# Another on-chip layout for the expert stage of a layer kernel, and another order of its 16 last x1 loads

## The reference

```python
x = x + layernorm(scan_layer(layernorm(x)))      # a state-space scan, 16 states per channel
x = x + layernorm(moe(layernorm(x)))             # 8 experts, top 2, and a shared expert

# moe, for each of the two choices k:
    pos = running count of the tokens that chose expert e;  keep = pos < 640
    h = gelu(buf @ w1[e] + b1[e]);  y = h @ w2[e] + b2[e] + gelu(buf @ wd[e]) @ wu[e]
    out += y[token's slot] * keep * weight
out += 0.2 * (gelu(x @ sw1 + sb1) @ sw2 + sb2 + gelu(x @ swd) @ swu)
```

## Time and profile before

| | us |
|---|---|
| median of 3 runs | 3554.31 (3552.27 to 3554.70) |
| the profiled execution | 3554.31 |
| its span, first to last instruction | 3552.6 |
| TensorE busy | 3143.4 (88%) |
| VectorE busy | 1853.6 (52%) |
| ScalarE busy | 1425.1 (40%) |
| GpSimd busy | 1727.5 (49%) |

### The profile page before, as it was taken

One profiled execution on the slowest core, in us unless ns is written; L12 is line 12 of the kernel. 1 busy time (PEld: TensorE's weight loads), 2 busy tenths in 40 slices (PEclk: granted clock), 3 DMA queues, 4 the chain that ended last, 5 costly groups with the idle time before them and its releaser, 6 DMA issues.

```text
span 3552.6 us, 43069 instructions
## 1 busy us (share of the span) xinstructions
PE 3143.4 (88%) x15191; PEld 2576.9 (73%) x15191; DVE 1853.6 (52%) x2708; ACT 1425.1 (40%) x2529; POOL 1727.5 (49%) x1577
## 2 busy tenths in 40 slices
PE   6455699988999988889999999999999999999991
PEld 3233577777777776678888888888888888888881
DVE  6699989988899981462322232223222322232225
ACT  7554676666766763312221321322313213223113
POOL 1087787987879874432341532613514416235102
PEclk8655799999999999879999999999999999999996
DMA  8859688696886945821230321412303314123036
GB/s 260 246 167 246 176 224 215 207 267 181 233 215 207 269 139 174 265 68 22 66 80 16 95 63 26 112 27 63 84 15 93 65 18 115 32 60 83 16 83 225
DMA packets 276920, 463.42 MB, mean 130 GB/s; under 512 B 32065, under 2 KB 107729, under 8 KB 276706
## 3 DMA queue, kind: packets, MB, share of 16 engines
q1 hardware_dynamic: 206656, 266.21, 26.5%
q0 software_dynamic: 68288, 194.06, 21.1%
q10 hardware_dynamic: 1762, 0.40, 0.1%
HBM read 363.44 MB, written 97.14 MB: 130 GB/s over the span
## 4 chain that ended last, share of the span: by engine, by line
PE 53%; DVE 2%; DMA 2%; issue 1%; POOL 1%; ACT 1%; SPq 0%; POOLq 0%; DVEq 0%; ACTq 0%
PE c_psH L1774 26%; PE c_psY L1818 25%; PE c_psT L1765 1%; PE c_psT L1869 1%; DMA raw<-in_w 1%; DVE d_y L1745 1%; DVE d_st L1729 1%; PE c_psY L1814 0%; DVE yst L1541 0%; DMA xrow<-x_d 0%; DMA acc_d<-yst,slot_lists 0%; POOL W1l L1411 0%; POOL acc_d L1456 0%; POOL W2l L1411 0%; ACT h L1325 0%
## 5 line engine op out<-in xcount | busy, mean ns | idle before, releaser
L1557 DVE CAST hh<-h 128x512 fp32r<-128x512 f32 (+1 forms) x400 | 177.0, 443 | 1257.1 <-ACT h L1331 1227.2
L1331 ACT ACTIVATE h<-c_psH,biases 128x512 f32<-128x512 f32 (+1 forms) x400 | 248.2, 621 | 1283.7 <-PE c_psH L1774 1260.1
L829 POOL TENSOR_TENSOR u<-dtxs,Bt 128x512 f32<-128x512 f32 x512 | 659.1, 1309 | 167.5 <-DVE b_psA L732 146.9
L732 DVE TENSOR_TENSOR_SCAN b_psA<-b_psA,b_few,u 128x512 f32<-128x512 f32 x512 | 656.9, 1283 | 63.8 <-ACT b_psA L602 61.2
L937 PE MATMUL b_psY<-ident,pr 128*128 128x128 f32 x2048 | 349.8, 310 | 210.7 <-DVE pr L739 192.1
L1818 PE MATMUL c_psY<-W2h,hh 128*128 128x512 f32 x1344 | 535.0, 398 | 0.6
L1818 PE MATMUL c_psY<-W2l,hh 128*128 128x512 f32 x1344 | 525.7, 391 | 0.0
L1818 PE MATMUL c_psY<-W2h,hl 128*128 128x512 f32 x1344 | 524.6, 390 | 0.0
L1416 POOL DMA_INDIRECT xrow<-xt_d,slot_lists x80 | 91.8, 1147 | 843.5 <-PE c_psT L1765 442.3
L937 PEld LDWEIGHTS b_psY<-ident,pr 128*128 128x128 f32 x2048 | 268.1, 157 | 295.1 <-DVE pr L739 242.6
L739 DVE TENSOR_TENSOR pr<-b_psA,Ct 128x512 f32<-128x512 f32 x512 | 354.3, 692 | 19.8 <-DMA Ct<-bc_d 2.0
(11 more groups left out here) (260 smaller groups left out, 5826.2 us busy)
## 6 DMA issues: line engine op xcount, KB each, us to landing
w<-ws_d POOLq DMA_DIRECT2D x224, 512.0 KB, 6.3
raw<-in_w SPq DMA_DIRECT2D x256, 256.0 KB, 2.8
Bt<-bc_d SPq DMA_DIRECT2D x64, 512.0 KB, 15.5
Ct<-bc_d SPq DMA_DIRECT2D x64, 512.0 KB, 19.6
xn<-in_x SPq DMA_DIRECT2D x8, 1024.0 KB, 6.9
xT_d<-xnT SPq DMA_DIRECT2D x8, 1024.0 KB, 8.4
dt_d<-a_dt SPq DMA_DIRECT2D x8, 1024.0 KB, 7.3
dtx_d<-a_dx SPq DMA_DIRECT2D x8, 1024.0 KB, 7.6
```

The lines of the kernel that those rows point to most:

```text
L732: nc.vector.tensor_tensor_scan(psA[q][:, :], psA[q][:, :], u[g % U_RING][:, :], carry[:, k:k + 1], ALU.mult, ALU.add).then_inc(s_h, 1)
L829: nc.gpsimd.tensor_tensor(u[g % U_RING][:, :], dtx[s % 2][:, :], Bt[n // TG][:, n % TG, :], ALU.mult)\
L1331: nc.scalar.activation(h32[:, 0:n * P], psH[j % 2][:, 0:n * P], ACT.Gelu, bias=b1[:, j - 1:j]).then_inc(s_gelu, 1)
```

## The change

It has two parts. First, the tiles of `experts` are opened in another order. The small tiles and Xb now come first, then the router's scratch tiles (closed again), and over the same bytes Xa, Xc and then the four weight tiles; after those are closed the tail's statistics tiles, `x1r` and `y` are laid over Xa, Xc and the weights together. The first byte of the tiles in a partition, summed up from the declarations:

| tile | before | after |
|---|---|---|
| L1h / L1l | 224,512 / 226,176 | 17,664 / 19,328 |
| Xbh / Xbl | 148,736 / 156,928 | 23,040 / 31,232 |
| Xah / Xal | 199,936 / 208,128 | 73,600 / 81,792 |
| Xch / Xcl | 216,320 / 220,416 | 89,984 / 94,080 |
| W1h / W1l | 17,664 / 50,432 | 98,176 / 130,944 |
| W2h / W2l | 83,200 / 115,968 | 163,712 / 196,480 |
| x1r[0] | 17,664 | 75,008 |
| y[0] | 83,200 | 140,544 |
| ident, the identity for transposes | 16,512 | 16,512 |
| skip_diagonal, of `mix` | 17,664 | 17,664 |

`x1r[0]` to `x1r[4]` now lie over Xa and Xc, `x1r[5]` begins in Xcl and reaches into W1h, `x1r[6]` to `x1r[12]` lie in W1h, `x1r[13]` lies across W1h and W1l, `x1r[14]` and `x1r[15]` in W1l. Second, the waits of SyncE in front of the loads of `x1r` follow this: groups 0 to 4 wait for the end of block 1, group 5 for 3 finished `up` of the last block, group 6 for 5, and so on to group 11 for 15, and groups 12 to 15 for all 17. The loads of `y` and their waits stay.

```diff
--- before.py
+++ after.py
@@ -1037,13 +1037,9 @@
         def sb(name, shape, dt=F32, where=ctx):
             return where.enter_context(nc.sbuf_tensor(name, shape, dt))
 
-        loop = ExitStack()
-        W1h, W1l = (sb(f"W1{h}", [P, FC, DT, P], F32R, loop) for h in "hl")
-        W2h, W2l = (sb(f"W2{h}", [P, FC, D], F32R, loop) for h in "hl")
-        loop.close()
-        x1r, y = ([sb(f"d_{n}{g}", [P, TAIL_G, D]) for g in range(NT // TAIL_G)] for n in ("x1", "y"))
+        L1h, L1l = sb("L1h", [P, DT, L3 + E], F32R), sb("L1l", [P, DT, L3 + E], F32R)
+        L2 = sb("L2", [L3, D], F32R)
         Xb = (sb("Xbh", [P, DT, 512], F32R), sb("Xbl", [P, DT, 512], F32R))
-        L2 = sb("L2", [L3, D], F32R)
         h32 = sb("h32", [P, 512])
         hh = [sb(f"hh{q}", [P, 512], F32R) for q in range(2)]
         hl = [sb(f"hl{q}", [P, 512], F32R) for q in range(2)]
@@ -1051,6 +1047,13 @@
         xrow = [sb(f"xrow{q}", [P, D]) for q in range(2)]
         yst = [sb(f"yst{q}", [P, D]) for q in range(4)]
         b2bc = sb("b2bc", [P, D])
+        biases = sb("biases", [P, (E + 2) * FC])
+        b1T, b1e = biases[:, 0:(E + 1) * FC], biases[:, (E + 1) * FC:(E + 2) * FC]
+        slots = sb("slot_rows", [P, 2, E * ST])
+        slot_g, slot_s = slots[:, 0, :], slots[:, 1, :]
+        few = sb("slot_lists", [P, LINE])
+        idx, sidx = few[:, 0:ST].bitcast(I32), few[:, ST:2 * ST].bitcast(I32)
+        wsl = few[:, 2 * ST:3 * ST]
         rt = ExitStack()
         OH = sb("OH", [P, K, NT, E], F32, rt)
         RA = sb("RA", [P, K, NT, E], F32, rt)
@@ -1073,20 +1076,16 @@
         hl_f = RA[:, :, :, :].rearrange("p k t e -> p (k t e)")[:, 0:2 * K * NT]\
             .rearrange("p (h k t) -> p h k t", h=2, k=K)
         rt.close()
-        end = ExitStack()
-        st, mv = (sb(f"d_{n}", [P, NT, m], F32, end) for n, m in (("st", 6), ("mv", 2)))
-        sd, rs, nm = (sb(f"d_{n}", [P, NT], F32, end) for n in ("sd", "rs", "nm"))
-        end.close()
-        Xa = (sb("Xah", [P, DT, 512], F32R), sb("Xal", [P, DT, 512], F32R))
-        X = (Xa, Xb, (sb("Xch", [P, DT, 256], F32R), sb("Xcl", [P, DT, 256], F32R)))
-        L1h, L1l = sb("L1h", [P, DT, L3 + E], F32R), sb("L1l", [P, DT, L3 + E], F32R)
-        biases = sb("biases", [P, (E + 2) * FC])
-        b1T, b1e = biases[:, 0:(E + 1) * FC], biases[:, (E + 1) * FC:(E + 2) * FC]
-        slots = sb("slot_rows", [P, 2, E * ST])
-        slot_g, slot_s = slots[:, 0, :], slots[:, 1, :]
-        few = sb("slot_lists", [P, LINE])
-        idx, sidx = few[:, 0:ST].bitcast(I32), few[:, ST:2 * ST].bitcast(I32)
-        wsl = few[:, 2 * ST:3 * ST]
+        loop = ExitStack()
+        Xa = (sb("Xah", [P, DT, 512], F32R, loop), sb("Xal", [P, DT, 512], F32R, loop))
+        X = (Xa, Xb, (sb("Xch", [P, DT, 256], F32R, loop), sb("Xcl", [P, DT, 256], F32R, loop)))
+        W1h, W1l = (sb(f"W1{h}", [P, FC, DT, P], F32R, loop) for h in "hl")
+        W2h, W2l = (sb(f"W2{h}", [P, FC, D], F32R, loop) for h in "hl")
+        loop.close()
+        st, mv = (sb(f"d_{n}", [P, NT, m]) for n, m in (("st", 6), ("mv", 2)))
+        sd, rs, nm = (sb(f"d_{n}", [P, NT]) for n in ("sd", "rs", "nm"))
+        x1r = [sb(f"d_x1{g}", [P, TAIL_G, D]) for g in range(NT // TAIL_G)]
+        y = [sb(f"d_y{g}", [P, TAIL_G, D]) for g in range(NT // TAIL_G)]
 
         low1 = [xrow[0][:, k * P:(k + 1) * P] for k in range(HOT)]
         high1 = [xrow[1][:, k * P:k * P + E * ST] for k in range(HOT)]
@@ -1258,10 +1257,11 @@
             for e in range(1, E):
                 load_pieces(e + 1, weights_of(e))
                 bias2(e, expert(e, 0))
-            for pair in range(FC // 2):
-                sp.wait_ge(s_mm1, expert(E - 1, 2)["B"] * J + 2 * pair + 3)
-                for g in (pair, pair + FC // 2):
-                    sp.dma_start(x1r[g][:, :, :], tail_rows(x1_d, g)).then_inc(d_x1[g], 16)
+            for g in range(NT // TAIL_G):
+
+                G = expert(E - 1, 2)["B"] * J
+                sp.wait_ge(s_mm1, G if g < 5 else G + min(J, 2 * g - 7))
+                sp.dma_start(x1r[g][:, :, :], tail_rows(x1_d, g)).then_inc(d_x1[g], 16)
             sp.wait_ge(s_mm2, E * 3 * J + J)
             for i in range(4):
                 sp.wait_ge(s_yst[i], added(E, i))
```

## The result

| | before | after |
|---|---|---|
| median, us | 3553.29 (3551.05 to 3554.70, 4 runs) | 3584.19 (3581.85 to 3588.78, 4 runs) |
| span of the profiled execution | 3552.6 | 3587.0 |

What follows compares the result with a forecast made beforehand. TensorE's products were taken to bound the expert stage and VectorE's steps the tail. Earlier loads, first five, last four, layout and preload, each 0, left 3554.3 us; range 3551 to 3559.

Steps and rivals of the forecast that it cites:

- The layout … I take 0: Expert stage: moving Xa, Xc and the weights to 128 beyond a multiple of 256 leaves the products' pace unchanged, 0.
- The first comparison: Stationary operands L1l (128 beyond) and L1h (none): 394 ns both with Xah, 396 against 393 with Xb; taken as 0.
- +3 ns: Difference of L1l against L1h with Xb, 396 against 393 ns; on all 8832 products 26 us, held as a rival's end.
- The second comparison: Moving operands ident (128 beyond), 273 ns, and skip_diagonal (none), 275 ns: a difference of −2 ns, taken as 0.
- The rival: Expert stage: weights or tokens 128 beyond a multiple of 256 slow each product, adding 26 us to 3581; chance 0.05.
- Loads earlier: Loads of x1r start earlier, but nothing waited for x1r before the tail's first addition: gain 0.
- the first five: Five x1r loads after block 1, 6.6 us long, in idle transfer time with 11 us of cover: 0.
- the last four: Four x1r loads behind the last wait, done about 1.2 to 1.7 us before the first scatter is written out: 0.
- the preload: Shared expert's weights loaded into moved tiles while TensorE is busy: 0, at most 0.9 us.
- The tail: VectorE's steps after the expert stage keep following each other every 2.87 us a group.
- What it named as proof of error: Expert-stage TensorE busy time changing over 7 us, last scatters landing later than 15 us after the last product, or VectorE awaiting d_x.

Runs made afterwards that it cites:

- m3_micro: No layer computed, TensorE alone: 104-column weights at steps of 512 or 416 bytes, then 128 moving columns; 226.7 ns matched, 228.9 to 231.7 with 104 columns.
- r2_all_odd: Kernel before with slot_lists opened first in the expert stage, so every large tile there starts 128 bytes beyond a multiple of 256; 3551.70 us, ratio 1.0002.
- r3_w_odd: Kernel before with slot_rows and slot_lists opened earlier, so only the four weight tiles start 128 bytes beyond a multiple of 256; 3587.07 us, ratio 1.0095.
- r1_even: Changed kernel with slot_lists opened behind the weights, so Xa, Xc and the weights start at multiples of 256 again; 3553.31 us, ratio 0.9998 to before.
- m1_micro: No layer computed, TensorE alone: 22 cases of 48 products with varied remainders by 256 of moving and weight tiles; 226.7 ns at equal remainders, 233.4 at 64.
- m2_micro: No layer computed, TensorE alone: matching with own or next weights, period and widths; 228.3 ns with only own weights matched, 230.0 with only the next.
- r7_w_64: r1_even with an unused 64-byte tile ahead of the router's scratch, so Xa, Xc and the weights start 64 beyond a multiple of 256; 3573.86 us, ratio 1.0055.

## Why the prediction was wrong

- **The step that failed is "The layout … I take 0".** It was the only term mis-sized: 0 in the forecast, 33.7 us by the steps of TensorE's products in the two profiled executions, and 31 us by the medians. The question was put rightly: the remainder by 256 was seen to change for Xa, Xc and the weights and to stay for Xb, `hh` and `hl`. The two comparisons that answered it with 0 could not see the price.
- *The first comparison* set L1l against L1h as two places, one off and one not. Their slices follow each other every 416 bytes, so both are mixed with the moving tile in most of their slices. m3_micro puts them at 230.6 and 231.7 ns: two slow cases compared. The "+3 ns" was no clean pair either: 396 is Xbh with L1l and 393 is Xbl with L1h, so the moving tile changed too; Xbh with L1h, in the same view, took 394. That view also had the hint, matched products with W1 of 389 ns against 393 to 396 for L1; I did not ask why. Part of that gap is the width of 104 columns (2.2 ns in m3_micro).
- *The second comparison* used products of 128 columns. At that width matched and mixed are alike (111.6 against 111.7 ns), as they are at 256, so it could not show what 512 columns pay.
- *The form of the question* was the deeper fault: I asked whether a place is slow, for one operand at a time. r2_all_odd moves every operand and costs nothing; r3_w_odd moves one and costs 34 us. What counts is a relation between two tiles, and I had written down which of them move and which stay without asking about the pair.
- *The rival* had the right time, 3581 us against 3584, and the wrong mechanism, "128 beyond a multiple of 256 costs": by that, r2_all_odd would have been slow. That the time came near is luck: its 3 ns, from the pair that was not clean, on 8832 products stand against 3 to 6 ns on 7296 wide ones, and the 1536 narrow ones paid nothing. Its chance of 0.05 came from the two blind comparisons, and the range followed it.
- *Loads earlier, the first five, the last four, the preload: 0.* Right. r1_even has all of them except the preload's moved remainder, and the time of before. The first wait came right at the end of block 1, and the gap between the last four loads and the end of the first scatter's writing out was about 1.8 us where 1.2 to 1.7 were forecast. The preload's tiles lie 128 bytes off in r2_all_odd, which is not slower: the rule of the Trainium skill on transactions from 256-byte boundaries (page "DMA: Bandwidth & Descriptors", section "How a descriptor splits into AXI transactions") has no price in this kernel's time that can be told. The transfers themselves do show one near the estimate: from 1454 to 1500 us GpSimd's packets of 2 KB took 99 ns in the mean before and in r1_even, 103 in r2_all_odd and 104 after the change, 4 to 5% more where the rule gave 6%. The 2 KB packets of SyncE from 1700 to 3380 us, nearly all of them loads of `raw` (where the weights land before they are split), show none: 84 ns in the median before, where `raw` starts at a multiple of 256, and in r2_all_odd, where it starts 128 beyond one.
- *The tail: 2.87 us a group.* Right.
- *What it named as proof of error* was what appeared: TensorE's busy time, over 7 us more.

The Trainium skill gives TensorE two read ports, one for the moving operand and one for the weights, which it calls independent (page "SBUF — State Buffer", section "Who interferes with whom"). Read plainly, that leaves a layout no way to change a product. m1_micro differs, 226.7 against 233.4 ns by the placement of two tiles alone, and the measurement decides.

What stays open: the mechanism, and whether it is a collision of reads at all, since neither the pair of a product with its own weights nor that with the next ones explains m2_micro by itself; why d = 192 is so much cheaper than d = 64; and whether other types than the four-byte ones used here pay it. Theory A's first half, reads that get in each other's way, and a conflict of banks behind it are guesses that no run here tests; what is shown is the price of the relation between the two places.

## What to carry to other kernels

When tiles are placed by a stack, a small tile opened or moved shifts all that follows, and a kernel bound by TensorE can lose 1% by that alone: compare the first bytes of weights and moving tiles by 256 before and after a change of layout, and keep them equal, also from slice to slice. If the mean of a full-width product shifts by a few nanoseconds everywhere with no wait added, look there first. And before two rows are used as proof that a price is zero, check that one of them is free of it.

## What the runs showed of the hardware

- With 512 moving columns of four bytes and 128 weight columns at the 2.4 GHz level, a product takes 226.7 ns from start to start when weights and moving tile start at the same remainder by 256, 229 when the weights are 192 beyond the moving tile, 232.4 at 128, and 233.4 at 64.
- With 384 columns the price for d = 128 is 2 to 3 ns; in the micro runs it is nothing with 256 columns (118.7 against 120.0 ns) and with 128 (111.7 against 111.6).
- The steps of mixed products repeat in a short pattern (236 and 231 ns in turn with d = 64), and matched products need a few steps to settle behind mixed ones: in m1_micro the case with both tiles at 128 began 236, 228, 233, 231 and then stayed at 226 and 227 ns. In the changed kernel the matched twelves of Xa, behind mixed ones with d = 128, took 2.76 us instead of 2.72; in r7_w_64, behind mixed ones with d = 192, they took 2.72.
- Preloads of 2 KB rows whose targets start 128 beyond a multiple of 256 took 103 to 104 ns a packet in the mean against 99 on GpSimd's queue, from 1454 to 1500 us.
